# Attention kernel: the sums leave by DMA, LayerNorm and the query parts move to GpSimd, one transposition less on TensorE

## The reference

```python
def _L0_attn_ref(x, W_down, tokeys, toqueries, tovalues, W_unify, b_unify):   # x: (8, 1024, 256), 16 heads of 16
    xd = (x @ W_down).reshape(b, t, h, s)
    keys = jnp.einsum('bthk,hik->bthi', xd, tokeys) * scale
    queries = jnp.einsum('bthk,hik->bthi', xd, toqueries) * scale
    values = jnp.einsum('bthk,hik->bthi', xd, tovalues)
    dot = jnp.einsum('bqhs,bkhs->bhqk', queries, keys)
    attn = jax.nn.softmax(dot, axis=-1)
    out = jnp.einsum('bhqk,bkhs->bqhs', attn, values).reshape(b, t, e)
    return out @ W_unify + b_unify
x = x + _L0_attn_ref(_layernorm(x, axis=-1), ...)
```

## Time and profile before

| | before |
|---|---|
| median of 3 runs | 2886.42 us (2884.84 to 2893.8) |
| the profiled execution, its own time | 2896.95 us |
| its span, first to last instruction | 2895.2 us |
| granted TensorE clock, mean | 0.964 |

### The profile page before, as it was taken

How to read it: one execution, slowest core, us unless ns; L and a number is a source line. 1 busy time by engine, 2 the same in 40 slices (tenths; PEclk the granted TensorE clock), 3 DMA queues, 4 the chain that set the end, 5 groups by cost and what they waited for, 6 DMA issues and landing times. The chain is left out here.

```text
span 2895.2 us, 48611 instructions
## 1 busy us (share of the span) xinstructions
PE 2705.7 (93%) x17009; PEld 1644.3 (57%) x17009; DVE 2145.9 (74%) x3552; ACT 1821.3 (63%) x3409; POOL 599.8 (21%) x562
## 2 busy tenths in 40 slices
PE   5899999867999999999999999999999589999997
PEld 3799999863334334333343343433433368999886
DVE  6555456747899898998998988989895665554574
ACT  5344556632777776777777767777777444444564
POOL 3355114521100100101001001010000235521353
PEclk9899999986999999999999999999999789999998
DMA  5211113414123132131231321312310512111341
GB/s 172 66 44 44 58 45 106 133 60 75 30 50 75 33 61 54 39 62 36 50 75 33 60 55 39 62 37 50 60 28 5 173 30 80 44 44 45 102 133 63
DMA packets 164529, 181.69 MB, mean 63 GB/s; under 512 B 38472, under 2 KB 133904, under 8 KB 164368
## 3 DMA queue, kind: packets, MB, share of 16 engines
q1 hardware_dynamic: 156176, 169.03, 24.0%
q0 software_dynamic: 8192, 10.57, 1.2%
HBM read 97.51 MB, written 31.54 MB: 45 GB/s over the span
## 5 line engine op out<-in xcount | busy, mean ns | idle before, releaser
L1457 ACT ACTIVATE at_ex<-at_pd 128x512 f32<-128x512 f32 x2048 | 1084.7, 600 | 383.7 <-PE at_pd L1360 379.2
L1521 DVE TENSOR_REDUCE at_mxc<-at_pb 128x2 f32<-128x1024 f32 x1024 | 1219.0, 1219 | 120.8 <-PE at_pb L1349 113.8
L768 DVE TENSOR_TENSOR f_ml_hl<-f_ml_h,f_ml_hh 128x512 fp32r<-128x512 f32 (+1 forms) x384 | 287.8, 751 | 422.7 <-ACT f_ml_hh L844 421.5
L1360 PE MATMUL at_pd<-at_qa,at_ka 50*128 50x512 f32 x2048 | 583.6, 469 | 3.9 <-ACT at_ex L1457 3.2
L1360 PEld LDWEIGHTS at_pd<-at_qa,at_ka 50*128 50x128 f32 x2048 | 266.6, 185 | 538.4 <-issue 349.2
L1369 PE MATMUL at_po<-at_ex,at_va 128*32 128x512 f32 x4096 | 548.8, 608 | 0.2 <-ACT at_ex L1457 0.2
L841 ACT ACTIVATE f_ml_h<-f_ml_pL,b1T 128x512 f32<-128x512 f32 (+1 forms) x384 | 243.8, 635 | 457.9 <-PE f_ml_pL L895 446.3
L1349 PE MATMUL at_pb<-at_ka,at_qa 48*128 48x512 f32 x2048 | 433.1, 450 | 24.7 <-DVE at_mxc L1521 16.5
L910 PE MATMUL f_ml_pA<-f_wh,f_ml_hh 128*128 128x256 f32 (+1 forms) x1408 | 410.4, 291 | 3.7 <-DVE f_ml_hl L768 3.7
L912 PE MATMUL f_ml_pA<-f_wl,f_ml_hh 128*128 128x256 f32 (+1 forms) x1408 | 402.5, 286 | 0.0
L913 PE MATMUL f_ml_pA<-f_wh,f_ml_hl 128*128 128x256 f32 (+1 forms) x1408 | 402.5, 286 | 0.0
(11 more groups left out here) (128 smaller groups left out, 2636.6 us busy)
## 6 DMA issues: line engine op xcount, KB each, us to landing
f_wraw<-in_L_ffn_w SPq DMA_DIRECT2D x128, 256.0 KB, 2.8
at_qa<-at_parts SPq DMA_DIRECT2D x384, 64.0 KB, 2.4
at_ka<-at_parts SPq DMA_DIRECT2D x384, 64.0 KB, 2.4
f_ro_xr<-in_L_attn_x SPq DMA_DIRECT2D x16, 512.0 KB, 3.9
f_ml_xr<-in_L_attn_x SPq DMA_DIRECT2D x16, 512.0 KB, 4.2
x<-f_ml_yo SPq DMA_DIRECT2D x16, 512.0 KB, 4.0
at_xr<-x SPq DMA_DIRECT2D x16, 512.0 KB, 5.1
at_xres<-x SPq DMA_DIRECT2D x8, 1024.0 KB
```

The lines of the kernel that those rows point to most:

```text
L768: eng.tensor_tensor(hl[h % RING][:, 0:w], h32[h % 2][:, 0:w], hh[h % RING][:, 0:w].bitcast(F32), ALU.subtract).then_inc(s_lo.sem, 1)
L1360: eng.matmul(pd[n % RING][:, :], ka[g][rows, p, kt * P:(kt + 1) * P], qa[g][rows, qh, p, :], start=True, stop=True).then_inc(s_full.sem, 1)
L1457: eng.activation(ex[t % 2][:, j, :], pd[n % RING][:, :], ACT.Exp).then_inc(s_free[n % RING].sem, 1)
L1521: eng.tensor_reduce(mxc[:, t // NT, kh, t % NT::NT], pb[kh][:, :].rearrange("p (e k) -> p e k", e=2), AX.X, ALU.max, negate=True).then_inc ...
```

## The change

- `values_out` goes from DVE to ACT, behind the exponentials of that step.
- Neither `f` nor `aT` remains in the steps. Pool writes `os_` to a DRAM tensor `oscr` (`sums_out`), reads the sums to `tot` and the weighted values straight to `aT` (`sums_in`), DVE takes the reciprocals of 16 numbers per partition in `tot` at steps 4 and 12, Pool writes them out (`totals_out`), reads them back spread over the 16 rows of each head (`totals_in`) and, once for each two units, multiplies (`divide`). All five DMAs of a half are on Pool's queue. `aT` now holds both halves.
- The last half of all is still turned on PE, at the end: one `f`, one `aT` (before: one `f`, two `aT`).
- The `u` tasks go to the next batch's first unit, at steps 2, 3, 11, 12; those of the last batch's first half to steps 14 and 15 of its last unit.
- LayerNorm: `apply` goes from DVE to Pool, a batch ahead (`normalize`, steps 7 and 10 of unit 2); statistics on DVE, a batch ahead too. Those of batch 1 are taken before the first step.
- `qk` is copied by ACT to `xT`, and both parts of the queries are made by Pool (`two_parts`), as the keys' are.

```diff
         def side_at(g, t, prev, last):
-            table = {1: ("f", 1), 9: ("f", 0)}
-            if g == 0 and not prev:
-                del table[1]
+            table = {}
             if g == 0 and prev:
-                table.update(zip((2, 3, 5, 6), OUT(1)))
-            if g == 3:
-                table.update(zip((10, 11, 13, 14), OUT(0)))
+                table.update(zip((2, 3, 11, 12), OUT(0) + OUT(1)))
+            if g == 3 and last:
+                table.update(zip((14, 15), OUT(0)))
...
@@ ScalarE
+            def values_out(b, g, t):
+                eng.wait_ge(s_pv.sem, s_pv.at(ST * unit(b, g) + t + 1))
+                if half(b, g, t // NT):
+                    eng.wait_ge(s_os.sem, s_os.at(16 * half(b, g, t // NT)))
+                eng.activation(os_[:, :], po[:, :], ACT.Copy).then_inc(s_o.sem, 1)
...
@@ VectorE
-            def values_out(b, g, t):
-                eng.wait_ge(s_pv.sem, s_pv.at(ST * unit(b, g) + t + 1))
-                eng.tensor_copy(os_[:, :], po[:, :]).then_inc(s_o.sem, 1)
+            def reciprocals(b, g, qh):
+                eng.wait_ge(s_td.sem, s_td.at(16 * (half(b, g, qh) + 1)))
+                eng.reciprocal(tot[:, :], tot[:, :]).then_inc(s_rc.sem, 1)
...
-                    if g == 0 and not last and t < 8:
-                        f, q = t // 4, t % 4
-                        if q < 2:
-                            stats(b + 1, f, (FIRST, SECOND)[q])
-                        else:
-                            apply(self.ring, b + 1, f, side, (FIRST, SECOND)[q - 2])
+                    if t == NT + 4:
+                        reciprocals(b, g, 0)
+                    if t == 4 and (b or g):
+                        reciprocals(*before(b, g), 1)
+                    if (g, t) in STATS_AT and b + 2 < NBAT:
+                        stats(b + 2, STATS_AT[g, t])
...
@@ GpSimd
+            def sums_out(b, g, qh):
+                eng.wait_ge(s_o.sem, s_o.at(half(b, g, qh) + 1))
+                eng.dma_start(oscr[g, qh, :, :, :].rearrange("j r q -> (j r) q"), os_[:, :]).then_inc(s_os.sem, 16)
+
+            def sums_in(ring, b, g, qh, read):
+                eng.wait_ge(s_os.sem, s_os.at(16 * (half(b, g, qh) + 1)))
+                eng.dma_start(tot[:, :], oscr[g, qh, :, HS, :].rearrange("j (x y) -> j x y", y=HS)).then_inc(s_td.sem, 16)
+                if b > 0:
+                    eng.wait_ge(s_full.sem, s_full.at(ring.full(read)))
+                r0 = HS * GH * (g % 2)
+                eng.dma_start(aT[r0:r0 + HS * GH, qh, g // 2, :], oscr[g, qh, :, 0:HS, :]).then_inc(s_nd.sem, 16)
+
+            def totals_out(b, g, qh):
+                eng.wait_ge(s_rc.sem, s_rc.at(2 + half(b, g, qh) + 1))
+                eng.dma_start(rscr[g, qh, :, :].rearrange("j (x y) -> (j x) y", y=HS), tot[:, :]).then_inc(s_rs.sem, 16)
+
+            def divide(b, g, qh):
+                eng.wait_ge(s_nd.sem, s_nd.at(16 * 2 * (half(b, g, qh) + 1)))
+                if g % 2:
+                    eng.tensor_tensor(aT[:, qh, g // 2, :], aT[:, qh, g // 2, :], den[:, qh, :],
+                                      ALU.mult).then_inc(s_dv.sem, 1)
```

More of the change, by code:

```diff
@@ L148, in tile_stats, with aggregate @@
         return last
+    def aggregate(self, eng, n, rows, tiles):
+        for j, r in enumerate(rows):
+            if j in tiles:
+                last = eng.bn_aggr(self.mv[0:r, j, :], self.stats[0:r, j, :])
+        return last
     def stats_step(self, eng, n, src, rows, tiles=range(4)):
@@ L155, in stats_step, with variance @@
         eng.memset(self.pad[:, :], 0.0)
-        for j, r in enumerate(rows):
-            last = eng.bn_aggr(self.mv[0:r, j, :], self.stats[0:r, j, :])
-        last.then_inc(self.s_dve.sem, 1)
+        self.variance(eng, n, rows, range(len(rows)))
+    def variance(self, eng, n, rows, tiles):
+        self.aggregate(eng, n, rows, tiles).then_inc(self.s_dve.sem, 1)
         eng.wait_ge(self.s_dve.sem, self.s_dve.at(3 * n + 2))
@@ L1218, in phase @@
                         a = self.place(task, b + 1, 1 - par, g)
-                    elif task == ("f", 1):
-                        a = self.place(task, *((b, par, g - 1) if g > 0 else (b - 1, 1 - par, 3)))
-                    elif task and task[0] in ("aT", "u") and g == 0:
+                    elif task and task[0] == "u" and g == 0:
                         a = self.place(task, b - 1, 1 - par, g)
@@ L1227, in phase, with units_landed @@
                     do.step(b, par, g, t, coming, tiles, done, a, side, ahead, last)
+        def units_landed(eng, b, c):
+            for g, p in ((0, 0), (0, 1), (1, 0)) if c == 0 else ((2, 0), (3, 0)):
+                eng.wait_ge(landed(g, p).sem, landed(g, p).at(loads(g, b)))
         block = ctx.enter_context(nc.Block())
@@ L1232, in _ @@
         def _(eng):
[L1233 removed]
+            for s in (*s_xr, *s_ld, *s_mr, s_ms, s_xl, *s_st):
                 s.open(eng)
@@ L1328, in end @@
                 def end(self, sides):
-                    for a in sides[3:]:
+                    for a in sides[2:]:
                         store_out(self.ring, a)
@@ L1682, in step @@
                 def step(self, b, par, g, t, coming, tiles, done, a, side, ahead, last):
-                    if g == 0 and not last and t in (1, 5):
-                        norm.pow_step(eng, 2 * (b + 1) + t // 4, 4)
-                    if a and a.kind == "xd":
-                        key_parts(self.ring, a)
-                    if g == 2 and t == 8:
+                    past = (b, g, 0) if t >= NT else (*before(b, g), 1) if b or g else None
+                    if past and t % NT == 0:
+                        sums_out(*past)
+                    if past and t % NT == 1:
+                        sums_in(self.ring, *past, self.read[past[2]])
+                    if past and t % NT == 5:
+                        totals_out(*past)
+                    if past and t % NT == 6:
+                        totals_in(*past)
+                    if g == 2 and t == 10 and b + 2 < NBAT:
+                        normalize(self.ring, b + 2, 1, side)
+                    if past and t % NT == 7:
+                        divide(*past)
+                    if g == 2 and t == 7 and b + 2 < NBAT:
+                        normalize(self.ring, b + 2, 0, side)
+                    if a and a.kind in ("xd", "qk"):
+                        two_parts(self.ring, a)
+                    if a and a.kind == "u":
+                        self.read[a.at[0]] = a.n
+                    if g == 3 and t in (2, 10):
                         eng.wait_ge(s_xl.sem, s_xl.at(16 * (8 + b + 1)))
-                        for q in range(0, NT, 2):
+                        for q in range(t // 8 * 4, t // 8 * 4 + 4, 2):
                             ins = eng.tensor_tensor(xres[:, q:q + 2, :], xres[:, q:q + 2, :],
```

280 lines of the change are left out of this document (149 added, 131 removed).

## The result

The changed kernel takes 2872.51 us (median of seven executions, six of them from 2865.2 to 2880.1). One execution at 4112.6 us, and one at 3524.4 in experiment 3, ran at a much lower clock (0.648) and are left out of the ratios. Against the kernel before the ratio is 0.9939 [0.9916, 0.9962]: some 17.6 us faster, where 46.6 were forecast and the range ended at 2866. The profiled execution is the median itself, 2872.51 us with a span of 2870.8 and a mean granted TensorE clock of 0.959 (0.964 before). That of before lay 10.5 over its median.

A forecast was written before the change was run, and what follows sets the result against it. A round through ACT was taken to set the 2.60 us step; terms -45.6, -9.1, +6.2, 0, +2.8, -1.9 and +1 sum to -46.6: 2850.3 us for the profiled execution, 2840 us as median, range 2828 to 2866.

The forecast's parts named there:

- What bounds a step: Attention steps without side task: a round through ACT, not PE alone, sets their length of 2.60 us.
- No `f`, no `aT`: Attention steps: 93 transpose tasks leave, each costing 0.49 us because it takes one of three banks; -45.6 us.
- LayerNorm off DVE: First unit of each batch: steps lengthened by DVE's statistics and normalisation become shorter; -9.1 us.
- The copy on ACT: Steps after a half's end: copying `po` on ACT delays the next exponential, 0.1 us for each of 62; +6.2 us.
- The rival of 32 us: Copy of `po` holds ACT's row for its whole 0.61 us: 2872 us; with like-sized Pool waits, 19 in 100.
- Sums and values through DRAM: Between halves: Pool's transfers land before DVE's reciprocal needs `tot`, with 5.8 us of cover, and Pool keeps up; 0 us.
- sums land late: Transfers of 7 us each make DVE's reciprocal wait: 2916 us; shares 13 in 100 with clock and unforeseen causes.
- The clock: Long runs of plain steps: PE granted 1.2 instead of 2.4 GHz, some 130 us a batch; within a shared 13 in 100.
- Start: Before the first `times_v`: Pool makes six pairs of parts ahead of the first head's load; +2.8 us (1 to 5).
- End: Behind the last half: one `aT` less; -1.9 us.
- Tail: Last unit: `u` waits for the quotient of the half before; +1 us (0 to 3).

The follow-up runs named there:

- experiment 3: `both_moved`: the changed kernel with Pool's bias additions at steps 5 and 13 of unit 3 and the second half of DVE's statistics four steps later; 2845.51 us, 0.9842.
- experiment 6: The kernel before with one transpose instead of four in each `f`, its result copied for the rest; 2884.09 us, one run.
- experiment 2: `stats_moved`: the changed kernel with the second half of DVE's LayerNorm statistics at steps 5 and 6 of unit 1 instead of 1 and 2; 2870.67 us, 0.9931.
- 9: The kernel of experiment 3 with one redundant product in each step of the last unit, to fill PE's idle time; 2842.05 us, 0.9839.
- experiment 10: The kernel of experiment 3 with the copy of `po` back on DVE and one redundant product in each step of the last unit; 2836.97 us, 0.9821.
- experiment 1: The changed kernel with Pool's additions of the bias to the residual at steps 5 and 13 of unit 3 instead of 2 and 10; 2848.52 us, 0.9861.
- experiment 5: The kernel before with Pool's four additions of the bias to the residual at unit 3 step 2 instead of unit 2 step 8; 2905.26 us, 1.0059.

## Why the prediction was wrong, step by step

- *What bounds a step* held: 2.60 us without side task, in both kernels, and the copy's place in the round gave 2.70.
- *No `f`, no `aT`*, -45.6: held, and so did its reason, the bank (experiment 6).
- *LayerNorm off DVE*, -9.1: the steps of 3.42 and 3.23 are gone. The sentence at its end, "DVE has less to do everywhere", is wrong: in unit 1 it has more to do, at a place where it already waited for Pool (5.1 us, experiment 2).
- *The copy on ACT*, +6.2: 0.09 in 56 steps (63, not 62, follow a half's end), 5.0 by the steps and 5.1 by the medians of 9 and 10. The rival of 32 us is refuted.
- *Sums and values through DRAM*, **0**: this is the step that failed. The five DMAs were judged rightly. DVE's reciprocal never waited for `tot` but once in the last unit, where DVE has nothing else to do. The transfers landed after 2.2 to 2.4 us (write of `oscr`, read of `tot`; the slowest write took 6.4) and 4.0 to 4.1 (`aT`, `den`), by the medians, so the rival "sums land late" falls. Pool's DMA takes 0.57 to 0.70 us of Pool, not the 1.0 counted. But I had asked of Pool's moved work only whether Pool would be late. I never asked what it would do to DVE while it runs. The additions had been in unit 2, away from a merge; moved to unit 3, onto the merge, they cost 24.8 us in the profile, and nothing again where experiment 1 took them off it. The wait was there to be read, in the kernel before: seven operations of 0.97 us in a group whose median is 0.18. I cited the page of the Trainium skill that has the rule, for descriptors, and passed over the rule that mattered.
- *The clock* was a rival, "hardly likely", on the strength of the earlier trace rows. No long run of plain steps with maxima fell. But behind four of the five steps that a stall had made longer than 4.1 us, and in the last unit where PE idles, TensorE ran at 1.2 GHz for one to six steps of up to 4.07 us. That is 10.1 of the 24.8 us, and 3.7 us in the very profile that the sum was made against; slices of 72 us can't rule it out.
- *Start* +2.8: 0.0 between the two profiles, but 4.6 when it is read from the right place. The first feed-forward part, which the change does not touch, ended 4.6 us later in the profile of before. These are its last operations on DVE, before and then after:

```profile
623.51 1.01 DVE L789 SCALAR_TENSOR_TENSOR f_ml_yo<-f_ml_pA,f_ml_xs 128x512 f32<-128x512 f32 x2 [1.63 <-PE f_ml_pA L913]
```

```profile
618.90 1.01 DVE L796 SCALAR_TENSOR_TENSOR f_ml_yo<-f_ml_pA,f_ml_xs 128x512 f32<-128x512 f32 x2 [1.63 <-PE f_ml_pA L920]
```

From their end to the first `times_v` it is 86.2 us before and 90.8 after. The other two profiles without the change have 86.7 and 86.2 (experiments 5 and 6), the nine others with it 90.1 to 91.0. Of the 4.6 us 4.0 lie between Pool's first part and the first product for maxima. So Pool's parts are the cost, as forecast, within the range of 1 to 5, and luck in the profile of before hid it.
- *End* -1.9: measured -2.7, of which 2.5 lie ahead of the second feed-forward part. *Tail* +1: 0.
- Together: the profile of after is 22.2 us over the 2850.3 forecast for it. The parts give 24.8 + 5.1 + 2.1 - 3.7 - 1.2 (copy) - 2.8 (start, as these two profiles have it) - 0.8 (end) - 1.0 (tail) = 22.5.
- The sum without the failed term was good: `both_moved`, the change with its Pool work out of the merge's way, has 45.6 us of the 46.6. That it is so near is in part luck: the start cost more than forecast and the copy less, and in the profiles the last unit lost 6.7 us to the lower clock there and 3.7 in before.

## To carry to other kernels

When work is moved to another engine, don't only ask whether that engine keeps up. Look at the maximum beside the median of each small operation on its neighbour: a few that are five times too long at one fixed place are a wait that slack still hides, and a map of where the next one will hurt. Small operations on the path deserve a place where the sharing engine is known to be quiet, by the order of its program, and not by chance timing of a DMA. And a profile can hold a lump of its own: read the steps' lengths through to the end before taking its span as the base of a sum.

## What the runs showed that I had not expected

- A DVE operation of 0.17 us waited up to 3.14 us for Pool. In experiment 5 it waited for the end of the addition that ran, the second or the third of four, and got in ahead of the next. With two additions it never got in between them. In five merges of after and six of `stats_moved` the operation began before the first addition had ended and lasted to the end of the second, 1.42 to 3.14 us. Four of the eleven began while Pool was still issuing the DMA `aT<-oscr` ahead of the additions, the others beside the first addition, as here (third batch of after):

```profile
1269.60 2.52 POOL L1771 TENSOR_TENSOR at_xres<-at_xres,at_bu 128x512 f32<-128x512 f32 x2
...
1270.34 1.82 DVE L1541 TENSOR_TENSOR at_nm<-at_mxc 128x16 f32<-128x16 f32 x1
```

Beside an issue of Pool's DMA alone such operations took 0.17 us in most cases and 0.39 at most (experiment 10). Why DVE gets in behind the second addition of four and not behind the first of two stays open.
- The five largest stalls of after, in which PE waited 1.4 to 2.4 us for DVE, made their step 1.5 to 3.2 us longer, and behind four of them 1.2 to 4.2 us more were lost by the clock.
- Step 1 of the first batch took 3.41 to 3.44 us in two profiles of kernels without the change and 4.06 in the third; with the change it took 3.98 to 4.07, and step 2 was long too in all but one, up to 4.07. The granted clock from 710 to 740 us of after is 0.85. No experiment was made on that.
